# Interleaved features in a projection's last body, and earlier halves of a reciprocal: one scheduling change in a decoder layer

## What is computed

```
qkv = layernorm(x) @ w_qkv                       # 16 heads of 32
q_proj = elu1(einsum("bhnd,hdf->bhnf", q, proj)) # 128 features a head
k_proj = elu1(einsum("bhnd,hdf->bhnf", k, proj))
kv     = einsum("bhnf,bhnd->bhfd", k_proj, v)
k_sum  = k_proj.sum(axis=2)
z      = 1 / (einsum("bhnf,bhf->bhn", q_proj, k_sum) + 1e-8)
x      = x + (einsum("bhnf,bhfd->bhnd", q_proj, kv) * z) @ w_out + b_out
```

## Time and profile before

| | |
|---|---|
| median of 3 runs | 2740.34 us (2738.92 to 2743.04) |
| profiled execution | 2736.47 us, its span 2734.7 us |
| mean granted TensorE clock | 0.968 of full speed |
| PE busy | 2585.5 us (95%) |
| DVE, ACT, POOL busy | 1307.3, 883.5, 352.9 us |
| projection's last body | 376.2 to 421.1 us |
| linear stage | 430.2 to about 790 us |

### The profile page before, as it was taken

The page is one execution under the profiler, slowest core; times in us unless marked ns, Lnnn a source line. Parts: engine busy times, 40 slices in busy tenths (PEclk is TensorE's granted clock), DMA queues, the critical chain, the costliest instruction groups (busy, mean ns, idle before and its releaser), DMA issues. The chain is left out here.

```text
span 2734.7 us, 34174 instructions
## 1 busy us (share of the span) xinstructions
PE 2585.5 (95%) x12680; PEld 1946.7 (71%) x12680; DVE 1307.3 (48%) x2027; ACT 883.5 (32%) x1411; POOL 352.9 (13%) x301
## 2 busy tenths in 40 slices
PE   7999987999979999999799999999998999999999
PEld 6888863665654555455478888888876888888887
DVE  4545535766636664566353333434344333343434
ACT  3555555767622222232221212111222121211121
POOL 1444452233210111011100000000000000000000
PEclk9999986999988999899989999999999999999999
DMA  6654544655321112112130000000123000000001
GB/s 194 165 134 122 139 97 119 197 143 165 109 93 47 62 71 78 47 62 102 73 146 24 23 23 23 23 23 23 46 95 113 24 23 23 23 23 23 23 23 61
DMA packets 67779, 207.00 MB, mean 76 GB/s; under 512 B 9968, under 2 KB 11760, under 8 KB 55664
## 3 DMA queue, kind: packets, MB, share of 16 engines
q1 hardware_dynamic: 67376, 204.81, 24.3%
q0 software_dynamic: 288, 0.69, 0.1%
HBM read 122.27 MB, written 58.72 MB: 66 GB/s over the span
## 5 line engine op out<-in xcount | busy, mean ns | idle before, releaser
L1914 PE MATMUL ex_pg<-ex_x,ex_w 128*128 128x512 f32 x3840 | 886.0, 390 | 3.3 <-DVE ex_lt L1797 3.3
L1914 PEld LDWEIGHTS ex_pg<-ex_x,ex_w 128*128 128x128 f32 x3840 | 723.5, 188 | 154.1 <-issue 3.5
L1929 PE MATMUL ex_pd<-ex_w,ex_ht 128*128 128x512 f32 x1920 | 446.6, 389 | 0.0
L1863 DVE TENSOR_TENSOR ex_h<-ex_s_g,ex_pg 128x512 f32<-128x512 f32 x160 | 110.0, 687 | 649.3 <-PE ex_pg L1914 648.4
L1929 PEld LDWEIGHTS ex_pd<-ex_w,ex_ht 128*128 128x128 f32 x1920 | 360.4, 188 | 74.8
L1770 ACT ACTIVATE ex_s_g<-ex_pg 128x512 f32<-128x512 f32 x160 | 95.8, 599 | 748.8 <-PE ex_pg L1914 748.7
L1835 DVE SCALAR_TENSOR_TENSOR ex_acc<-ex_pd,ex_share,ex_acc 128x512 f32<-128x512 f32 x320 | 234.2, 747 | 90.4 <-PE ex_pd L1929 85.0
L584 PE MATMUL pr_pj<-pr_xt,pr_w 128*128 128x512 f32 x768 | 189.4, 405 | 1.4 <-DVE pr_xt L472 1.4
L378 POOL TENSOR_TENSOR pr_ks_sum<-pr_ks_sum,pr_kp 128x512 f32<-128x512 f32 x128 | 165.0, 1289 | 178.5 <-DVE pr_kp L501 166.9
L584 PEld LDWEIGHTS pr_pj<-pr_xt,pr_w 128*128 128x128 f32 x768 | 148.6, 196 | 32.9 <-DVE pr_xt L472 1.8
L1301 ACT ACTIVATE cr_ring<-cr_s_bank 128x512 f32<-128x512 f32 x160 | 95.7, 598 | 202.9 <-PE cr_s_bank L1525 202.9
(11 more groups left out here) (176 smaller groups left out, 2815.2 us busy)
## 6 DMA issues: line engine op xcount, KB each, us to landing
stage<-in_units SPq DMA_DIRECT2D x21, 1536.0 KB, 6.4
qk<-pr_kq SPq DMA_DIRECT2D x192, 128.0 KB, 2.4
qk<-q_scratch SPq DMA_DIRECT2D x96, 256.0 KB, 4.4
q_scratch<-pr_kq SPq DMA_DIRECT2D x128, 128.0 KB, 2.3
x_scratch<-cr_x SPq DMA_DIRECT2D x16, 1024.0 KB, 4.2
pr_x<-in_x SPq DMA_DIRECT2D x8, 1024.0 KB, 5.6
li_x<-in_x SPq DMA_DIRECT2D x8, 1024.0 KB, 7.7
x_scratch<-li_x SPq DMA_DIRECT2D x8, 1024.0 KB, 3.9
```

Source lines behind the costliest of these rows:

```text
L1863: nc.vector.tensor_tensor(h[:, f], s_g[:, f], pg[2 * f + 1][:], ALU.mult).then_inc(h_set, 1)
L1914: mm = nc.tensor.matmul(pg[2 * f + which][:], w[:, slot, sp_, col:col + P], x3[:, m, k, c * TB:(c + 1) * TB], start=(n == 0), stop=(n == 3 ...
L1929: mm = nc.tensor.matmul(pd[t][:], ht[:, s % 2, sp_, f, t * P:(t + 1) * P], w[:, slot, m, WD + f * D:WD + (f + 1) * D], start=(n == 0), sto ...
```

## The change

In the last body TensorE issues the next group's features one by one behind this group's sums, instead of all four ahead of the next piece. In the linear stage the two reciprocal casts on ScalarE are moved forward, POOL computes both low halves before it adds bias to two tiles, and VectorE casts `spread` in the last slot of body -1 instead of the first.

```
-                        for t in range(TT if i >= 0 else 0):
-                            features(i, TT * g + t)
+                        if 0 <= i < LAST or i == LAST and g == 0:
+                            for t in range(TT):
+                                features(i, TT * g + t)
                         for key, lo, hi in PLANS[i][g]:
                             piece(key, lo, hi)
                         for t in range(TT if i >= 0 else 0):
                             kv(i, TT * g + t)
+
+                            if i == LAST and g + 1 < G:
+                                features(i, TT * (g + 1) + t)
...
+                    reciprocal_low(i, 0)
+                    reciprocal_low(i, 1)
                     add_bias(i, 0)
-                    reciprocal_low(i, 0)
                     add_bias(i, 1)
-                    reciprocal_low(i, 1)
...
                         if now and s == 0 and h == 1:
                             take_den(i)
+                        if now and s == 1 and h == PER + 1:
+                            reciprocal_high(i, 1)
...
                         take_num(i, G - 1)
+                    if now and s == 0:
+                        reciprocal_high(i, 0)
                     if behind and s == 0:
                         query(i - 1, 0)
-                    if now and s == 1:
-                        reciprocal_high(i, 0)
+                    if now and s == 1 and not ahead:
                         reciprocal_high(i, 1)
...
-                    if i == -1 and s == 0:
+                    if i == -1 and s == SLOTS - 1:
                         dve.wait_ge(const_in, 48)
                         nc.vector.tensor_copy(spread[:], spread_raw).then_inc(spread_set, 1)
```

## The result

The changed kernel takes 2712.24 us (median of 4 runs, 2708.45 to 2716.24), the kernel before beside it 2739.63 (2737.03 to 2743.04). The ratio is 0.9897 with a 95% interval of 0.9881 to 0.9914, so 28 us less, 24 to 33. A second series of the same kernel gave 2714.44 against 2741.48, ratio 0.9906 (0.9889 to 0.9922). The profiled execution is the fastest of its series, 2708.45 us with a span of 2706.6, which will matter: its last body turns out to be one of the two shortest of five.

The account below looks back on a forecast made before the run. TensorE, working nearly through the whole span, was taken as the bound. Terms -13.4 - 5.6 - 9.5 = -28.5 us took the profiled 2736.5 to 2708.0; the runs' median lies 3.9 above, so 2712; range 2703 to 2723.

Parts of the forecast that it names:

- The last body: Projection's last body: interleaved features fill TensorE's idle times, periods of 7.5 us at full clock; -13.4 us.
- I take full clock: Last body: the granted clock no longer falls behind the 12 matmuls; if the tax stays, -5.3 us instead of -13.4.
- Rival 1: Last body: the clock swings on, so that part is -5.3 us and the whole 2720 us; chance 0.17.
- The spread cast: Linear stage's start: with the cast in the eighth slot the first bend comes 6.05 us earlier; -5.6 us net.
- The reciprocal's halves: Linear stage: POOL's wait of 2.50 us goes, L934 holds next, 1.25 us gained per steady block; -9.5 us in all.
- Rival 2: Linear stage: L934 doesn't hold L1059, so the whole wait goes, -17.8 us for -9.5, 2703.5 us; chance 0.06.
- rivals 3: Linear stage: the wait only changes its name, L934 as late as before, reciprocal part 0, 2721 us; chance 0.08.
- 4: Whole change does nothing: the trace names wrongly what holds the sums' adds and the bend; 2740 us; chance 0.04.
- rival 5: Linear stage: slower, ScalarE's wait for the second reciprocal (lead 0.35 us) delays fourth head and queries; 2746 us; chance 0.03.

Follow-up runs that it names:

- body_only: The kernel before with only the last body's new order of features: 2732.89 us, ratio 0.9967 to the kernel before.
- cast_only: The kernel before with only the spread cast moved to the eighth slot: 2736.47 us, ratio 0.9978 to the kernel before.
- norm_first: The changed kernel with VectorE's four normalisations (L941) ahead of the fifth head's add in slot 2: 2704.30 us, ratio 0.9867 to the kernel before.
- recip_only: The kernel before with only the reciprocal's halves moved on ScalarE and POOL: 2727.79 us, ratio 0.9945 to the kernel before.
- casts_behind_old_order: As casts_behind, but with the features in one piece again, the interleaving undone: 2701.74 us, ratio 0.9859 to the kernel before.
- casts_behind: The changed kernel with ScalarE and VectorE taking the last body's query cast behind all four features instead of two: 2699.50 us, ratio 0.9849 to the kernel before.
- both: The changed kernel with the edits of norm_first and casts_behind together: 2691.72 us, ratio 0.9824 to the kernel before.

## Why the prediction was right

The time was forecast at 2712 and came out at 2712.24, but two of its three terms were off the mark in opposite directions, in part because of the clock. That they cancelled to 0.3 us is luck; what was earned is the direction, the range and the waits.

- **The last body, -13.4.** The mechanism is as worked out: 7.53 us for a period of 7.5, 6.67 unchanged, 0.67 us of idle at the third sum for 0.4 to 1.1. The idle of some 0.4 forecast ahead of the fourth sum is none. The step that failed is "I take full clock". In the profiled execution it fell once, and the body won 11.7; over the profiles of either order it wins 8.8, and `body_only` 9.0 in time. Rival 1 (-5.3) is what two of five executions show. The argument that the stretch behind the 12 matmuls has twice the work was true (2.52 us of the 3 from 382.00 in the new profile, for 0.68) and didn't suffice.
- **The spread cast, -5.6.** The bend came 6.0 us earlier as forecast. It measured -5.0 alone and -4.0 in the changed kernel, where the third block of sums fell on the low clock; `cast_only` gave -6.0 in time (3.3 to 8.8).
- **The reciprocal's halves, -9.5.** The next bound was named rightly: the fourth pair of matmuls, held by the bank that L941 reads. The add came at 528.58 and L941 0.61 behind it. Blocks are 41.15 - 39.93 = 1.22 us shorter for 1.25, and `norm_first` shows that it was this order on VectorE. Missing was that behind the 2.50 us of idle the clock is low in some executions, 3.5 us in two of four profiles, 1.8 on average, and in none of the 25 intervals of the new order. If the kernel before pays this average, one comes to about -11; `recip_only` measured -15 by the ratio (interval -11.5 to -18.9). Between 0.4 and 8 us of that I can't place; its own profile shows only -8.6 from the stage's first head to the last 48 query matmuls. From there to the end, through work that no edit touches, the four profiles with the wait of 2.50 us took 1957.8 to 1963.5 us and the eight others 1953.3 to 1957.5. Whether these 3 to 4 us belong to the reciprocal or to the scatter of executions no run here tells, and this stays open.
- **The sum.** Too much by 4 to 5 us in the body, too little by 2 or more at the reciprocal. The range 2703 to 2723 held both series of runs.
- **Rival 2** (the whole wait goes) became true only with L941 moved; **rivals 3** and **4** are out (blocks 1.22 us shorter, and every part won); **rival 5**: the second half is cast at 525.19, 0.35 us behind the end of the second reciprocal (524.84), so the lead is as calculated.
- The rule of the Trainium skill on short idle times between groups of matmuls ("TensorE: Matmul & The Clock Gate", section "A second HAM failure mode: psum-queue depth-cycling") agrees with the trace of the new last body: the clock fell in one to three of three places, with one idle time of 0.67 us ahead of each. It isn't borne out everywhere: `casts_behind_old_order` has an idle time of 0.65 to 0.68 us in each group and kept the clock. I had given that rival 0.17; with two of five executions near its size and one in between, it deserved about half.

## What to carry to other kernels

When an engine waits in the middle of a group, look first at what stands in front of the late instruction in its producer's own queue. Here moving one cast behind two features brought the last body from a mean of 45.8 us to 26.6 (one profile), rearranging TensorE's instructions only to 37.0, and both together to 25.6. When a wait before a set of matmuls is removed, count the banks they fill: with three banks the fourth output waits for the first one's reader, and it is that reader's place in its queue that sets the gain. One profile shows one draw of the clock: before a term is built on "the clock holds", profile the kernel more than once.

## What the runs showed of the hardware

In the first three groups of the new last body the clock fell although TensorE's longest idle time there was 0.67 us. In the windows of `body_only` it was busy by the profile for 2.59 us of the 3 us ahead of the fall and 2.62 of the 3 in which it came (the eighth column is the granted clock):

```profile
379.00:382.00 3.00, 2.59 (x28) 1.59 (x26) 1.18 (x2) 2.21 (x5) 1.31 (x2) 1.00 0.90 210
382.00:385.00 3.00, 2.62 (x25) 1.90 (x25) 1.64 (x4) 2.85 (x5) 2.58 (x3) 0.74 0.00 0
385.00:388.00 3.00, 3.00 (x9) 2.33 (x9) 0.64 (x1) 0.00 (x0) 2.49 (x2) 0.50 0.68 164
```

In the profile of the changed kernel, where the same matmuls start within 0.1 us of these, the clock stayed up in the same place, with about the same busy time in sum:

```profile
379.00:382.00 3.00, 2.68 (x28) 1.68 (x26) 1.09 (x2) 2.15 (x4) 1.40 (x2) 1.00 0.77 172
382.00:385.00 3.00, 2.52 (x27) 1.90 (x28) 1.68 (x3) 2.90 (x6) 2.49 (x2) 1.00 0.00 0
```

In `casts_behind` and `both` the same instructions without the idle time kept the clock in all four groups. But `casts_behind_old_order` kept it too, with the idle times of 0.65 to 0.68 us in every group, so the idle time alone doesn't decide it. And behind the same wait of 2.50 us ahead of L1059 the clock was low in 6 blocks of 24 and stayed up in 18, with nothing in their rows to tell them apart. So whether the clock is low behind a short idle time varied from execution to execution here, and what decides it stays open. It cost 1.0 to 1.4 us in a steady block and 1.6 us (9.11 for 7.53) to 3.1 us (10.64 for 7.53) in a group of the last body, and an average over executions is what a change to such a place wins.

In `casts_behind` TensorE was busy by the profile without a pause in the 32 two-column matmuls of the key sums (5.52 us from 402.36), and the granted clock went from 1.00 (402.36 to 403.36) to 0.71 and then 0.50 within them; the last idle time ahead, 1.08 us, had ended at 401.90. The prediction put their low clock down to the idle times ahead of the last two sums. These are gone in `casts_behind`, and the clock fell even so, some 1.5 us into these matmuls, where in the changed kernel they start at 0.50.
